# First normalization of a two-layer transformer block: rows of blocks 2 to 7 scaled and both turned halves copied by ScalarE, spread over six heads per block

## The chip, the cores and the metric

One NeuronCore of one Trainium2 chip runs the whole program. The metric is the device time of one execution in microseconds. A kernel is timed in several executions, and one more execution is taken with the hardware profiler; all rows below come from that one.

## What is computed

Two layers, each attention plus a mixture of experts on a normalized input, over 8 sequences of 512 tokens of width 256 (4096 rows). Cut to what matters here:

```python
def _layernorm(x, axis=-1, eps=1e-05):
    m = jnp.mean(x, axis=axis, keepdims=True)
    v = jnp.var(x, axis=axis, keepdims=True)
    return (x - m) / jnp.sqrt(v + eps)

# layer 0: 16 heads of 16, causal softmax over 512 tokens; 8 experts, 2 per token, plus a shared one
xn = _layernorm(x)
x = x + _L0_attn_ref(xn, Wq, Wk, Wv, Wo) + _L0_ffn_ref(xn, Wg, Wu, Wd, W1, W2)
# layer 1: gated recurrent attention over the sequence; 8 experts, 2 per token
xn = _layernorm(x)
x = x + _L1_attn_ref(xn, ...) + _L1_ffn_ref(xn, ...)
```

The change touches only the first `_layernorm`.

## The kernel before

The 4096 rows stay in on-chip memory (`ACC`) as 8 blocks of 4 tiles of 128 rows; block b is sequence b. Each sequence has two groups of eight heads, so the layer-0 attention is one loop over 128 heads, numbered by `idx`, in 16 groups `n = idx // 8`. After it come the layer-0 experts, the second layer's attention, and its experts.

The order of the attention stage is written out by hand. `attention_order` (it calls `attention_places` and `ln0_steps`) makes one list of steps, and every engine walks through that list and takes its own part of each step, strictly in order. For `idx` from -11 to 134 a turn holds, in this order: `scoresT` of head idx (TensorE computes the turned scores into banks 3 to 5, ScalarE takes the exponentials in two pieces, GpSimd masks them), the steps of `attention_places`, `scores` of head idx+11 (TensorE into banks 0 to 2, VectorE takes row maxima), `values` every fourth turn (TensorE, always into PSUM bank 6, copied out by ScalarE), and then one entry of `ln0_steps` or, when those are used up, one step of the expert routing (`route` 0 to 19 on VectorE, then 64 scatters on GpSimd). TensorE holds one head of each kind at a time: `scoresT` of a head waits for the exponentials of the head before it, `scores` for the maxima of the head before it.

The other steps of a turn repeat every eight heads: with k the group number, `project` (queries and keys of a later group, TensorE, then ScalarE and VectorE split the result) at turns 8k+2 and 8k+3, `unscaleT` at 8k+2, `scale` at 8k+1 and 8k+5 (TensorE turns, VectorE divides by the sums), `split` and `maxrow` at 8k+5 (VectorE cuts the maxima into three parts, TensorE turns them), and `output` or `project_v` at 8k+6 and 8k+7. `values` stands at 8k+4 and 8k+8.

The first normalization of blocks 0 and 1 comes ahead of the loop. For blocks 2 to 7 `ln0_steps` gives one step per turn, five turns a block: `norm` (VectorE `norm0`, L1924 to L1937: a reciprocal, then four scalings of 128x256 from `ACC` into `xn0`; SyncE L685 to L687 then stores the block to `XN`), `xt0` and `xt1` (TensorE `xt`, L1419 to L1425, turns half c of the block with four transposes; ScalarE L1139 to L1142 copies half 0 into `xnT`, VectorE L1939 to L1942 copies half 1), `logits` and `logitsT` (TensorE L1431 to L1444, VectorE copies at L1949 and L1954). The means and roots of blocks 2 to 7 are there before the loop reaches them. So block b has `norm` at turn 5b-15, `xt0` at 5b-14, `xt1` at 5b-13, `logits` at 5b-12, `logitsT` at 5b-11, and the routing starts at turn 25. All blocks from 2 on share one buffer `xn0`, so the scaling of block b waits until block b-1 is turned and stored.

PSUM banks for these short results come from `attention_banks`: a ring of four banks up to turn 0, and from turn 0 on (`two_banks`) a ring of banks 7 and 6, where each `xt0`, `xt1`, `logits`, `logitsT`, `project`, `project_v`, `maxrow`, `scale`, `unscaleT` and `output` takes the next one in turn. TensorE waits (`take`) until the last use of that bank is read. `values` always takes 6.

Of the kernel before, what the change touches and what calls it, by code (L numbers as in the profile page):

```python
# [45 lines left out]
def ln0_steps():  # L46

    yield []
    yield []
    yield [("stats", 6)]  # L50
    yield []
    yield [("stats", 7)]
    yield [("root", 2)]
    for b in range(2, NB):
        for kind in ("norm", "xt0", "xt1", "logits", "logitsT"):
            yield [(kind, b)]
# [245 lines left out]
def build(nc, t, out):  # L302
    ctx = ExitStack()
    with ctx:
# [261 lines left out]
        root = sem("root")  # L566
        normed = sem("normed")
        bank = {k: sem(f"bank{k}_read") for k in (4, 5, 6, 7)}
        turned = sem("xn_turned")
# [82 lines left out]
        def logits_read(b):  # L652

            return (bank[7], f4[3] + 2) if b == NB - 1 else (bank[6], f4[2] + 2 * b + 2)

        def rooted0(b):
            return b + 1 if b < 2 else 4


        def sync(sp):  # L660
# [24 lines left out]
            def norm0(b):  # L685
                sp.wait_ge(normed, 2 * b + 2)
                sp.dma_start(xnd[b], xn0[b]).then_inc(xn_out[b % 2], 16)  # L687
# [54 lines left out]
            for kind, *a in plan0:  # L742
                if kind == "norm":
                    norm0(*a)
                    if a[0] == 0:
                        late_loads()
                elif kind == "low":
                    split_out(*a)
# [359 lines left out]
        def scalar(act):  # L1108
# [29 lines left out]

            def xt0(b):  # L1139
                bk, use = banks0["xt0", b]  # L1140
                act.wait_ge(turned, 2 * b + 1)
                act.activation(xnT[:, 0, 512 * b:512 * b + 512], ps(bk, 0, 512), ACT.Copy).then_inc(bank[bk])  # L1142

# [70 lines left out]
            for kind, *a in plan0:  # L1214
                if kind == "stats" and a[0] >= 4:
                    stats0(*a)
                elif kind == "root":
                    root0(*a)
                    if a[0] == 0:
                        heads_last()  # L1220
                elif kind == "xt0":
                    xt0(*a)
                elif kind == "project":
                    project(*a)
                elif kind == "project_v":
                    project_v(*a)
                elif kind == "maxrow":
                    maxrow(*a)
                elif kind == "scoresT":
                    scoresT(*a)  # L1230
                elif kind == "values":
                    values(*a)
                elif kind == "shared_gelu":
                    shared_up(*a)
                elif kind == "first_gelu":
                    first_gelu(*a)
                elif kind == "first_down":
                    first_down(*a)
                elif kind == "unscaleT":
                    unscaleT(*a)  # L1240
                elif kind == "route" and a[0] == 0:
                    act.wait_ge(r_shift, 1)
                    act.activation(RR[0].A, RR[0].A, ACT.Exp).then_inc(r_exp)
# [168 lines left out]
        def tensor(pe):  # L1412
# [6 lines left out]
            def xt(b, c):  # L1419
                pe.wait_ge(normed, 2 * b + 2)  # L1420
                pe.wait_ge(cst_in, 32)
# [489 lines left out]
        def vector(dve):  # L1911
# [12 lines left out]
            def norm0(b):  # L1924
                dve.wait_ge(root, rooted0(b))
                dve.reciprocal(RS[:, 4 * b:4 * b + 4], RS[:, 4 * b:4 * b + 4]).then_inc(normed)
                dve.wait_ge(normed, 2 * b + 1)
                if b == 2:
                    dve.wait_ge(xn_out[0], 16)
                elif b > 2:  # L1930
                    dve.wait_ge(xn_out[(b - 1) % 2], 16 * ((b - 1) // 2 + 1))
                if b >= 2:
                    dve.wait_ge(turned, 2 * b)
                for j in range(4):
# [3 lines left out]

            def xt1(b):  # L1939
                bk, use = banks0["xt1", b]  # L1940
                dve.wait_ge(turned, 2 * b + 2)
# [572 lines left out]
```

## Time and profile before

| | us |
|---|---|
| median of 3 runs | 1647.87 (1644.03 to 1649.47) |
| profiled execution, its own time | 1642.28 |
| span of its trace | 1640.5 |

Over the span TensorE's matmuls are busy 1536.9 us (94%), VectorE 861.1 us (52%), ScalarE 733.3 us (45%), GpSimd 713.8 us (44%). The attention loop runs from about 34 us to 499 us, the layer-0 experts follow. The page names engines PE (TensorE matmul), PEld (its weight loads), DVE (VectorE), ACT (ScalarE), POOL (GpSimd), SP (SyncE). `L1936` is line 1936 of the kernel. In a row of the timeline the bracket at the end holds the idle time of the engine ahead of the piece and what ended it; in a row that holds several instructions the form printed is that of the first. In the windows each engine has its busy time with the instruction count in brackets; PEclk is the granted TensorE clock as a share of 2.4 GHz, DMA the busy share of the DMA engines. The windows of group 2 begin and end where a `values` step starts: 84.44 us is turn 4, 99.19 turn 8, then 12 at 113.64, 16 at 128.99, 20 at 144.51, 24 at 162.57, 28 at 179.57, 32 at 191.62, 40 at 216.72, 48 at 250.24.

### The profile page before, as it was taken

How to read it: one execution, taken by the hardware profiler on the slowest of the kernel's cores; microseconds unless marked ns; L12 is line 12 of the kernel's file. 1: busy time of each engine (PE TensorE's matmuls, PEld its weight loads, DVE VectorE, ACT ScalarE, POOL GpSimd, SP SyncE). 2: the span in 40 equal slices, each digit the busy share in tenths (PEclk: the TensorE clock that was granted, in tenths of full speed). 3: DMA queues.
4: the chain of work that ended last, by engine and by line, in shares of the span. 5: the costliest groups of instructions: out<-in, count | busy, mean ns of one | idle time of the engine just before them, and what ended most of it. 6: DMA issues, size and time to landing. Idle time of an engine off the chain costs nothing.

```text
span 1640.5 us, 32489 instructions
## 1 busy us (share of the span) xinstructions
PE 1536.9 (94%) x10874; PEld 1180.9 (72%) x10874; DVE 861.1 (52%) x2424; ACT 733.3 (45%) x1923; POOL 713.8 (44%) x815
## 2 busy tenths in 40 slices
PE   5888989999999999999988799998999999999997
PEld 3445445555547999998655467767999899999996
DVE  5777897787822444442577778874322122222220
ACT  4544545555551232333556466644333333334332
POOL 3132336676532555553810467753333333333332
PEclk9899999999999999999998999999999999999999
DMA  8534324435306444444622386467333333333331
GB/s 271 126 115 110 79 73 98 104 94 102 83 4 240 108 113 114 113 114 130 204 92 67 103 219 105 79 105 290 59 56 52 51 56 54 55 58 59 53 55 23
DMA packets 154640, 167.60 MB, mean 102 GB/s; under 512 B 84821, under 2 KB 132817, under 8 KB 151409
## 3 DMA queue, kind: packets, MB, share of 16 engines
q1 hardware_dynamic: 129936, 128.15, 31.5%
q0 software_dynamic: 24544, 37.38, 10.6%
q8 instruction: 94, 1.54, 0.4%
q14 instruction: 66, 0.53, 0.1%
HBM read 104.10 MB, written 44.45 MB: 91 GB/s over the span
## 4 chain that ended last, share of the span: by engine, by line
PE 78%; DVE 10%; DMA 4%; issue 3%; ACT 3%; SPq 1%; POOL 0%; another core or an unknown queue 0%; DVEq 0%; ACTq 0%; POOLq 0%
PE PS L1660 23%; PE PS L1678 22%; PE PS L1517 4%; PE PS L1453 3%; PE PS L1767 3%; DVE PS L1980 3%; PE PS L1502 3%; PE PS L1481 2%; PE PS L1634 2%; PE PS L1543 2%; PE PS L1588 2%; PE PS L1779 2%; PE PS L1463 1%; PE PS L1865 1%; DMA arena<-FD 1%
## 5 line engine op out<-in xcount | busy, mean ns | idle before, releaser
L1660 PEld LDWEIGHTS PS<-arena 128*128 128x128 f32 x3408 | 398.2, 192 | 16.3 <-DVE arena L2201 4.9
L1660 PE MATMUL PS<-arena 128*128 128x128 f32 x3408 | 405.3, 276 | 3.5 <-DVE arena L2201 3.5
L1678 PE MATMUL PS<-arena 128*128 x1704 | 392.3, 379 | 0.0
L1678 PEld LDWEIGHTS PS<-arena 128*128 128x128 f32 x1704 | 311.9, 190 | 40.1 <-issue 0.2
L1980 DVE CUSTOM_DVE_ANT_0 PS<-PS,arena 128x512 f32<-128x512 f32 (+3 forms) x512 | 235.2, 522 | 50.7 <-PE PS L1481 47.2
L995 POOL DMA_INDIRECT out<-arena x71 | 111.7, 1573 | 296.4 <-ACT arena L1272 274.0
L1262 ACT ACTIVATE arena<-PS,arena 128x128 f32<-128x128 f32 x568 | 161.8, 368 | 138.3 <-PE PS L1660 136.5
L2226 DVE COPY arena<-arena 128x8 f32 x71 | 12.2, 172 | 347.5 <-ACT arena L1262 326.3
L928 POOL TENSOR_SCALAR_AFFINE_SELECT arena<-arena 128x256 f32<-128x256 f32 x256 | 99.4, 411 | 204.0 <-ACT arena L1178 203.7
L981 POOL DMA_INDIRECT arena<-XN,arena x142 | 145.0, 1021 | 98.6 <-PE PS L1645 40.6
L1178 ACT ACTIVATE arena<-PS 128x512 f32<-128x512 f32 (+1 forms) x256 | 166.5, 705 | 42.1 <-PE PS L1502 34.4
L1272 ACT ACTIVATE arena<-PS,arena 128x256 f32<-128x256 f32 x142 | 67.3, 474 | 256.0 <-PE PS L1680 177.8
L2227 DVE COPY arena<-arena 128x1024 f32 (+1 forms) x142 | 136.5, 961 | 75.5 <-ACT arena L1254 59.4
L954 POOL DMA_INDIRECT SLOT<-arena x128 | 155.7, 1217 | 30.3 <-issue 30.3
L988 POOL DMA_INDIRECT SUM<-arena x71 | 70.2, 989 | 98.0 <-ACT arena L1272 98.0
L1481 PE MATMUL PS<-arena 96*128 96x512 bf16 (+3 forms) x512 | 100.3, 307 | 8.1 <-DVE arena L1980 5.7
L1502 PE MATMUL PS<-arena 99*128 99x512 bf16 (+3 forms) x512 | 97.5, 307 | 6.0 <-ACT arena L1178 5.3
L1254 ACT ACTIVATE arena<-PS 128x512 f32<-128x512 f32 x71 | 42.4, 597 | 115.3 <-issue 75.3
L1502 PEld LDWEIGHTS PS<-arena 99*128 99x128 bf16 x512 | 45.5, 99 | 56.7 <-issue 18.1
L2215 DVE COPY arena<-arena 128x512 uint16<-128x512 uint16 x126 | 53.7, 426 | 60.1 <-DMA arena<-XN,arena 59.1
L1481 PEld LDWEIGHTS PS<-arena 96*128 96x128 bf16 x512 | 49.1, 99 | 49.3 <-DVE arena L1980 16.5
L1517 PE MATMUL PS<-arena 128*32 128x512 f32 (+3 forms) x1024 | 75.7, 435 | 4.8 <-DVE arena L1966 3.6
(246 smaller groups left out, 2014.3 us busy)
## 6 DMA issues: line engine op xcount, KB each, us to landing
arena<-FD SPq DMA_DIRECT2D x32, 512.0 KB
arena<-in_w SPq DMA_DIRECT2D x16, 1024.0 KB
SPL<-arena SPq DMA_DIRECT2D x32, 384.0 KB, 2.6
arena<-SPL SPq DMA_DIRECT2D x64, 192.0 KB
XN<-arena SPq DMA_DIRECT2D x16, 512.0 KB, 3.0
arena<-SPL SPq DMA_DIRECT2D x64, 128.0 KB
arena<-SUM SPq DMA_DIRECT2D x16, 512.0 KB, 6.4
arena<-in_x SPq DMA_DIRECT2D x8, 512.0 KB, 6.6
```

What stands on the lines that cost most here:

```text
L954: pool.indirect_dma_start(SLOT[layer], bass.IndirectOffsetOnAxis(ap=POS[:, n, i:i + 1], axis=0), META[:, i, n, :], None).then_inc(row_out[ ...
L981: pool.indirect_dma_start(MOE[layer].xr[i % 4][:, :], None, XN, row).then_inc(tile_in[i % 4], 16)
L995: pool.indirect_dma_start(out, row, m.y[i % 3][:, :], None, compute_op=ALU.add).then_inc(y_out[i % 3], 16)
L1178: act.activation(PB[h % NPB][:, lo:hi], ps(3, lo, hi), ACT.Exp, scale=0.25).then_inc(p_made)
L1262: ins = act.activation(m.hT[i % len(m.hT)][:, 128 * f:128 * f + 128], ps(m.UPB[i % 2], 128 * f, 128 * f + 128), ACT.Gelu, bias=m.bias[i % ...
L1481: ins = pe.matmul(ps(0, o, o + w), q[0:96, j, 128 * i:128 * i + 128], k[0:96, j, 0:w], start=True, stop=True)
L1502: ins = pe.matmul(ps(3, o, o + w), k[0:99, j, 128 * kb:128 * kb + 128], q[0:99, j, 128 * kb:512], start=True, stop=True)
L1517: ins = pe.matmul(PS[32 * j:32 * j + 32, 6, 128 * kb:512], vb[:, kb, 8 * half + jj, :], PB[(8 * n + jj) % NPB][:, OFFT[kb]:OFFT[kb] + w], ...
L1660: ins = pe.matmul(o, m.now[i % 2][:, c * F + 128 * f:c * F + 128 * f + 128], m.xt[i % 2][:, 128 * c:128 * c + 128], start=(c == 0), stop=( ...
L1678: ins = pe.matmul(to, m.hT[i % len(m.hT)][:, 128 * c:128 * c + 128], m.WD[:, bass.ds(e * (nf * 256) + c * 256, 256)], start=(c == 0), stop ...
L1980: dve.tensor_tensor_reduce(sc, sc, MASK[:, 384 - 128 * r:512], -1.0, -NEG, ALU.add, ALU.min, NM[n % 2][:, r, j:j + 1]).then_inc(s_max)
L2227: dve.tensor_copy(m.now[i % 2][:, :], m.WU[:, bass.ds(e * m.wrow, m.wrow)]).then_inc(w_staged)
```

## The change

Blocks 0 and 1 stay as they are. For blocks 2 to 7 VectorE's `norm0` keeps the reciprocal and adds one small operation that makes NB1 = -mean x 1/deviation; the four scalings are now ScalarE activations (`ACT.Identity` with per-row scale and bias), two per turn in two turns, called `scaled` 0 and 1. ScalarE also copies half 1 of the turned block. A block now takes six turns instead of five: `norm` and `scaled` 0 at 6b-17, `scaled` 1 at 6b-16, `xt0` at 6b-15, `xt1` at 6b-14, `logits` at 6b-13, `logitsT` at 6b-12; the routing starts at turn 31. The waits for the store and for the turning of the block before move from VectorE to ScalarE. TensorE and SyncE wait for the new semaphore `scaled0` instead of `normed`, and SyncE stores a block at `scaled` 1.

```diff
@@ ln0_steps
     for b in range(2, NB):
-        for kind in ("norm", "xt0", "xt1", "logits", "logitsT"):
+        yield [("norm", b), ("scaled", b, 0)]
+        yield [("scaled", b, 1)]
+        for kind in ("xt0", "xt1", "logits", "logitsT"):
             yield [(kind, b)]
@@ build
+        def normed0(b):
+            return (normed, 2 * b + 2) if b < 2 else (scaled0, 2 * b - 2)
@@ sync
             def norm0(b):
-                sp.wait_ge(normed, 2 * b + 2)
+                sp.wait_ge(*normed0(b))
                 sp.dma_start(xnd[b], xn0[b]).then_inc(xn_out[b % 2], 16)
...
-                if kind == "norm":
+                if kind == "norm" and a[0] < 2:
                     norm0(*a)
...
+                elif kind == "scaled" and a[1] == 1:
+                    norm0(a[0])
@@ scalar
-            def xt0(b):
-                bk, use = banks0["xt0", b]
-                act.wait_ge(turned, 2 * b + 1)
-                act.activation(xnT[:, 0, 512 * b:512 * b + 512], ps(bk, 0, 512), ACT.Copy).then_inc(bank[bk])
+            def xt(b, c):
+                bk, use = banks0[f"xt{c}", b]
+                act.wait_ge(turned, 2 * b + 1 + c)
+                act.activation(xnT[:, c, 512 * b:512 * b + 512], ps(bk, 0, 512), ACT.Copy).then_inc(bank[bk])
+
+            def scaled(b, half):
+                act.wait_ge(normed, 2 * b + 2)
+                act.wait_ge(turned, 2 * b)
+                if b == 2:
+                    act.wait_ge(xn_out[0], 16)
+                else:
+                    act.wait_ge(xn_out[(b - 1) % 2], 16 * ((b - 1) // 2 + 1))
+                for j in (2 * half, 2 * half + 1):
+                    i = 4 * b + j
+                    ins = act.activation(xn0[b][:, j, :], ACC[:, i, :], ACT.Identity, bias=NB1[:, i:i + 1], scale=RS[:, i:i + 1])
+                ins.then_inc(scaled0)
...
-                elif kind == "xt0":
-                    xt0(*a)
+                elif kind == "xt0" or kind == "xt1" and a[0] >= 2:
+                    xt(a[0], int(kind[2]))
+                elif kind == "scaled":
+                    scaled(*a)
@@ tensor
             def xt(b, c):
-                pe.wait_ge(normed, 2 * b + 2)
+                pe.wait_ge(*normed0(b))
@@ vector
                 dve.wait_ge(normed, 2 * b + 1)
-                if b == 2:
-                    dve.wait_ge(xn_out[0], 16)
-                elif b > 2:
-                    dve.wait_ge(xn_out[(b - 1) % 2], 16 * ((b - 1) // 2 + 1))
                 if b >= 2:
-                    dve.wait_ge(turned, 2 * b)
+                    dve.scalar_tensor_tensor(NB1[:, 4 * b:4 * b + 4], MV[:, 4 * b:4 * b + 4, 0], -1.0, RS[:, 4 * b:4 * b + 4], ALU.mult, ALU.mult).then_inc(normed)
+                    return
...
             def xt1(b):
+                if b >= 2:
+                    return
```

## Rows read from the trace of the kernel before

**Rows 1.** The profile's page: span and busy time by engine

```profile
span 1640.5 us, 32489 instructions
PE 1536.9 (94%) x10874; PEld 1180.9 (72%) x10874; DVE 861.1 (52%) x2424; ACT 733.3 (45%) x1923; POOL 713.8 (44%) x815
```

**Rows 2.** Windows: length, then busy PE, PEld, DVE, ACT, POOL; PEclk, DMA, GB/s

```profile
84.44:99.19 14.75, 11.98 (x82) 6.79 (x82) 11.64 (x48) 7.53 (x12) 4.31 (x10) 0.78 0.45 141
...
144.51:162.57 18.06, 15.96 (x112) 10.55 (x113) 12.24 (x48) 6.32 (x11) 3.99 (x9) 0.81 0.34 104
162.57:179.57 17.00, 14.48 (x82) 6.43 (x82) 12.06 (x49) 7.62 (x14) 4.32 (x9) 0.90 0.30 76
...
216.72:250.24 33.52, 27.89 (x174) 15.50 (x173) 28.91 (x106) 14.32 (x25) 12.60 (x21) 0.90 0.30 71
...
287.22:311.73 24.51, 23.27 (x168) 13.26 (x169) 18.99 (x77) 14.28 (x25) 16.13 (x27) 1.00 0.45 98
```

**Rows 3.** Timeline of TensorE, turns 1 to 8: start, length, line, idle before

```profile
70.49 0.38 PE L1502 MATMUL PS<-arena 99*128 99x512 bf16 x1 [1.03 <-ACT arena L1178]
...
72.78 1.12 PE L1424 MATMUL PS<-arena 128*128 128x128 f32 x4 [0.64 <-DVE arena L1936]
...
87.61 0.30 PE L1444 MATMUL PS<-arena 128*128 128x128 f32 x1 [0.81 <-ACT arena L1184]
...
93.03 1.11 PE L1424 MATMUL PS<-arena 128*128 128x128 f32 x4 [1.96 <-DVE arena L1936]
...
96.07 1.06 PE L1424 MATMUL PS<-arena 128*128 128x128 f32 x4
```

**Rows 4.** The same timeline, turns 12 to 45

```profile
116.80 0.63 PE L1424 MATMUL PS<-arena 128*128 128x128 f32 x4 [0.80 <-ACT arena L1184]
...
118.36 0.60 PE L1525 MATMUL PS<-arena 128*128 128x128 f32 x4
...
121.46 0.64 PE L1437 MATMUL PS<-arena 128*32 128x128 f32 x16 [2.10 <-DVE arena L2004]
...
150.97 1.09 PE L1424 MATMUL PS<-arena 128*128 128x128 f32 x4 [2.10 <-DVE arena L2004]
...
174.46 3.65 PE L1453 MATMUL PS<-arena 128*128 128x512 f32 x4 [0.35 <-DVE arena L1966]
...
240.17 0.60 PE L1489 MATMUL PS<-arena 128*24 128x128 bf16 x4 [2.11 <-DVE arena L1993]
```

**Rows 5.** The same timeline, in a stretch without normalization or routing on VectorE

```profile
311.73 2.36 PE L1517 MATMUL PS<-arena 128*32 128x512 f32 x32 [0.36 <-DVE arena L1966]
...
317.73 1.97 PE L1543 MATMUL PS<-arena 128*128 128x256 f32 x8 [0.38 <-DVE arena L2004]
319.54 0.71 PE L1502 MATMUL PS<-arena 99*128 99x512 bf16 x4
```

**Rows 6.** Timeline of VectorE around the normalization of block 7

```profile
146.28 1.38 DVE L1936 TENSOR_SCALAR arena<-arena 128x256 f32<-128x256 f32 x4
```

**Rows 7.** Groups by line, 60 to 200 us: VectorE and ScalarE forms that the change concerns

```profile
L1178 ACT ACTIVATE arena<-PS 128x768 f32<-128x768 f32 x35 | 28.4, 812 | 0.1
...
L1936 DVE TENSOR_SCALAR arena<-arena 128x256 f32<-128x256 f32 x20 | 7.5, 435 | 0.2
...
L1942 DVE COPY arena<-PS 128x512 f32<-128x512 f32 x6 | 4.1, 685 | 2.6 <-PE PS L1424 2.6
```

**Rows 8.** Timeline of ScalarE: the second layer's normalization, the same form of activation

```profile
791.42 2.08 ACT L1314 ACTIVATE arena<-arena 128x256 f32<-128x256 f32 x4 [2.21 <-DVE arena L2273]
793.40 1.05 ACT L1199 ACTIVATE arena<-PS 128x512 f32<-128x512 f32 x2
794.47 1.28 ACT L1378 ACT_TABLE_LOAD   x1
```

**Rows 9.** The lines of the second layer's per-row scaling and its small VectorE operation

```profile
L1314 ACT ACTIVATE arena<-arena x32: 584/588/602, 791.4 to 862.6; 128x256 f32<-128x256 f32 x32
...
L2273 DVE SCALAR_TENSOR_TENSOR arena<-arena x8: 161/164/2452, 789.8 to 860.9; 128x4 f32<-128x4 f32 x8
```

More of the change, by code:

```diff
@@ L567, in build @@
         normed = sem("normed")
+        scaled0 = sem("scaled0")
         bank = {k: sem(f"bank{k}_read") for k in (4, 5, 6, 7)}
```

## The prediction

> **What bounds the kernel now.** I read the page first [rows 1]: matmuls are busy 94% of the span, so time can only come from gaps of TensorE or from its clock. Then windows over the attention loop [rows 2]. A stretch with neither normalization nor routing needs 24.51 us for eight heads, with TensorE busy 23.27 of it at full clock. While blocks 4 to 7 are normalized, the four-head windows take 14.75, 18.06 and 17.00 us; all six from turn 4 to turn 28 take 179.57 - 84.44 = 95.1 us, where three quiet periods would take 73.5. Granted clock falls there too: 0.78, 0.81, 0.90. Third, TensorE's own timeline, for what ended its gaps. At 93.03 it waited 1.96 us for the scalings of block 4 (L1936), at 72.78 0.64 us for those of block 3 [rows 3]. At 121.46 and 150.97 it waited 2.10 us each for `scale` on VectorE (L2004), the second time behind the scalings of block 7, which stand 4 us earlier in VectorE's queue [rows 4, 6]. At 87.61 and 116.80 it waited 0.8 us for ScalarE's copy of the `values` bank, since a short step had drawn bank 6 too [rows 3, 4].
>
> A gap costs twice. After the gap before 93.03, one turning of a half with a `scoresT` and a `scores` takes 96.07 - 93.03 = 3.04 us; the same three take 118.36 - 116.80 = 1.56 us elsewhere [rows 3, 4]. That is 1.2 instead of 2.4 GHz, and it lasts two such rounds, so it costs some 3.0 us on top of the gap. The same follows the gaps before 72.78, 150.97 and 240.17 (0.6, 2.1, 2.1 us), and at 174.46 four matmuls of projections take 3.65 us, some 1.8 of it the slow clock if that doubles them too, after gaps of 0.3 [rows 3, 4]. So VectorE's queue at normalization is on the path although VectorE is busy 52% over the span.
>
> **What the change removes, adds and moves.** VectorE loses per block four scalings of 0.435 us by the mean (1.38 us in a row, they overlap) and one copy of 0.685 us, and gains one small operation of 0.16 us [rows 6, 7, 9]: some 1.9 us less per block, 11.5 us over six. ScalarE gains 2.08 us for four scalings of this very form, and about 0.53 us for the copy, as two such copies in a row take 1.05 [rows 8]: 2.6 us per block, 15.7 us over six. It is busy 6.3 to 7.6 us in those windows of 14.8 to 18.1 us [rows 2], so there is room. TensorE's and SyncE's instructions stay the same in number; they move to later turns.
>
> *ScalarE's new wait.* ScalarE now waits, at turn 6b-17, for a VectorE operation queued behind the maxima of that turn, and the exponentials of the next head are queued behind it. Let TensorE end that turn's `scores` at t. VectorE ends its share by t + 2.3 at most (9.3 us for four heads, being 11.64 busy less the scalings and the copy [rows 2, 7]), the two small operations end at t + 2.7, two scalings at t + 3.7, the next exponentials (0.81 and some 0.55 us) at t + 5.1. TensorE meanwhile does the next `scoresT` and, held by the same maxima, the next `scores`, and is through at about t + 2.5. What covers the rest is the long step of the next turn. The turns 6b-16 are 2, 8, 14, 20 and 26 for blocks 3 to 7, and each holds one: `project` at 2 and 26, `project_v` at 14 (1.8 us as at 319.54 - 317.73 [rows 5]), `values` at 8 and 20 (2.4 us [rows 5]). That leaves a gap of about 0.2 to 0.8 us per block, mostly shorter than those before. Without that cover it would be 2 to 2.6 us.
>
> *Sum, turns 4 to 28.* Three quiet periods are 73.5 us. Heads 6 and 7 have no `output` or `project_v` yet, less 2 x 1.8 = 3.6: 69.9. In turns 5 to 8 VectorE's 9.3 us are then longer than TensorE's 12.3 - 3.6 = 8.7, and with small gaps I take 1.3 more: 71.2. TensorE's normalization work in these turns is 8 turned halves of about 0.5 us (0.63 less the overlap with the next piece), 4 `logits` of about 0.58 (0.64 less overlap) and 4 short turnings of 0.1 [rows 4]: 6.7, together 77.9. The new waits above take 0.5 us in each of five places: 2.5. That TensorE never falls to 1.2 GHz in this stretch is too much to ask; before it did at 93, 151 and 174 us, and I leave one such fall of 3.0 in. That makes 83.4, so 11.7 us less than 95.1. Without any fall it is 14.7; with all three left, 5.7.
>
> *What is paid back.* One turned half, a `logits` and a short turning of block 7 move behind turn 28: 1.2 us. Routing step 0, a chain between VectorE and ScalarE, moves from turn 25 to turn 31. Before, its window lost 17.00 - 14.48 = 2.5 us in gaps and those 1.8 us in slow projections [rows 2, 4]; not all of it is the chain's. Between 0.7 and 4.2, I take 2.0 us. Together 3.2.
>
> *Before turn 4.* The scalings of block 2 leave VectorE just before the first maxima are cut, for which TensorE waits. This is worth between nothing and their 1.38 us [rows 6]; I take 1.0, since at block 4 the whole length showed.
>
> *Banks.* From turn 0 on the short results alternate between 7 and 6. `logitsT` of block 2 now falls into turn 0, so all later steps draw the other bank. Before, the second `project` of a period had bank 6, and `values`, always bank 6, waited 0.36 us for VectorE to read it [rows 5]. That wait recurs each eight heads. After, the last user of bank 6 ahead of that `values` is `unscaleT`, read long before. Twelve periods from turn 32 on give at most 4.3 us; as 0.38 us at L1543 [rows 5] shows that VectorE is close behind at other places, I take 3.5, and nothing as the other end.
>
> *Routing steps 15 to 19* now lie at turns 46 to 50, not 40 to 44. Their window takes 33.52 us, 9.0 more than a quiet period, part of it a fall of the clock after 240.17 [rows 2, 4]. VectorE's work in them is unchanged. I take no change, with 3 us to either side. The 64 scatters end at turn 114 instead of 108, still before the loop's end, so they cost nothing; if they ran past it, six of them of about a turn each would show.
>
> The sum: 1.0 + 11.7 + 3.5 - 3.2 = 13.0 us. The profiled execution of 1642.3 becomes 1629.3; it was 5.6 us below the median of 1647.9, so on the median I predict **1634.9 us**.
>
> **A rule against the change.** The row of the same form shows 0.588 us for a ScalarE scaling [rows 9], VectorE's takes 0.435 us [rows 7], so the moved work grows by a third. The Trainium skill, page "ScalarE: Activation LUTs", section "Rules for kernel authors", says just this: additions and multiplications belong on VectorE. Were ScalarE's time on the path, the 24 scalings would cost 24 x 0.15 = 3.7 us more instead of saving 10. By the windows it is not, so the sum does not follow the rule.
>
> **The rivals.**
>
> *More goes than I think.* The falls at 93, 151 and 174 all vanish, and that before 72.78, which follows gaps of 1.03 us on ScalarE and 0.64 us on the scalings [rows 3], goes too. That is 6 us more: about 1629.
>
> *Only the direct gaps go.* Other gaps take over as the cause of the slow clock, as the heads have a lead of only one over VectorE. What remains is 1.96 + 0.64 + about 1.4 at 150.97 and part of the bank effect: 5.5 us, less 3.2 paid back, or 1642 to 1646. For it: two of the 2.1 us waits end at L2004, not at the scalings. Against: that L2004 is late by the scalings in the same queue.
>
> *ScalarE's wait becomes the gap (slower).* At each 6b-17 the exponentials of the next head stand behind VectorE, TensorE waits 2 to 2.6 us (the figure without cover) and falls to half clock for another 3.0: about 5.3 us for each of five blocks, 26 us against 13. That gives 1661. It decides from 13.0 / 5 = 2.6 us per block on. For it: gaps of 2 us and a slow clock do go together in every case above. Against: a long TensorE step follows each of the five places.
>
> *A table load per scaling.* If `ACT.Identity` were not in the table that the exponentials use, each turn with scalings would add two loads of 1.28 us [rows 8]. Ten turns in the loop with half of it on the path are 13 us, which cancels the gain: 1648 to 1660. The row shows the scalings and then a Gelu with no load between them, but no row shows them between exponentials.
>
> *It does not do what it says.* If the scalings of a block were late for its `xt0`, TensorE would wait there as before. They end over a turn ahead of it, so this has no chance of its own.
>
> **Chances.** The forecast, 1630 to 1641: 0.52. More: 0.12. Direct gaps only: 0.24. ScalarE's wait: 0.09. Table loads: 0.03. About 0.3%, or 4.9 us, is what a measurement of this kernel can tell from no change, so faster means below 1643.0. From the forecast, the larger gain and half of the third case: 0.76. Same, 1643.0 to 1652.8: the other half of the third and some of the last two, 0.15. Slower: 0.09. The range takes in the bounds of routing, banks and clock falls: 1624 to 1647.
>
> **What the profile would show.** No L1936 row after block 1, and ScalarE rows of 128x256 in pairs, without a table load beside them. TensorE's turnings at full clock, with no gap over 1 us before them. The six windows from turn 4 to 28 together near 83 us, a quiet period near 24.2 us, and no wait of `values` for VectorE's L1966 in it. The routing window would still be some 9 us too long. I am wrong if TensorE's gaps are ended by the exponentials right after the `scaled` turns, if the clock in the windows is still about 0.8, or if the quiet period is unchanged.

## The result, and the profile after

The changed kernel takes **1625.07 us** (median of 4 runs, 1620.84 to 1626.41); the kernel before, run beside it, 1645.95 us (median of 4, 1639.79 to 1649.47). The ratio is 0.989 with a 95% interval of 0.986 to 0.992; by the ratio the gain is 18 us, 13 to 23 by its interval, so the 13.0 that I had predicted lie at its edge. The profiled execution took 1625.28 us, that of before 1642.28. I had predicted 1634.9: the direction was right, the gain between the medians was 20.9 us instead of 13.0. The forecast's own band, 1630 to 1641, did not hold it; the range, 1624 to 1647, did.

The page of the kernel after answers to [rows 1] (busy time, its share of the span, instructions):

```profile
span 1623.5 us, 32501 instructions
PE 1525.4 (94%) x10874; PEld 1171.9 (72%) x10874; DVE 847.0 (52%) x2400; ACT 747.1 (46%) x1953; POOL 714.1 (44%) x815
```

VectorE lost 14.1 us and ScalarE gained 13.8, near the 11.5 and 15.7 that I had worked out. TensorE executes the same 10874 matmuls in 11.5 us less: most of the 17 us by which the span is shorter is clock, not gaps.

The windows of after, turns 4 to 28 in steps of four heads, then turns 28 to 32, the window with routing (turns 44 to 52), and a quiet one (turns 56 to 64); columns as in [rows 2]:

```profile
77.58:89.75 12.17, 9.84 (x95) 5.07 (x94) 10.05 (x44) 6.41 (x12) 4.37 (x10) 1.00 0.38 118
...
117.71:131.78 14.07, 12.77 (x103) 6.88 (x102) 9.81 (x39) 7.49 (x13) 4.12 (x9) 1.00 0.54 111
131.78:147.13 15.35, 12.96 (x113) 8.38 (x113) 11.65 (x46) 9.71 (x18) 4.12 (x9) 1.00 0.44 132
147.13:160.49 13.36, 12.76 (x86) 6.40 (x85) 10.22 (x41) 9.14 (x17) 3.86 (x9) 1.00 0.44 108
160.49:174.50 14.01, 12.33 (x110) 8.16 (x109) 10.76 (x43) 7.75 (x14) 4.38 (x10) 1.00 0.33 96
...
211.04:243.14 32.10, 27.23 (x173) 14.09 (x173) 29.96 (x124) 15.13 (x26) 9.57 (x19) 0.95 0.34 88
255.12:279.00 23.88, 23.15 (x169) 13.03 (x168) 18.94 (x77) 14.01 (x25) 16.15 (x26) 1.00 0.46 103
```

The third column from the right is the granted clock. It is 1.00 in every window up to turn 32, where [rows 2] had 0.78, 0.81 and 0.90. Turns 4 to 28 in one window, before and after:

```profile
84.44:179.57 95.13, 81.69 (x590) 46.27 (x590) 70.21 (x275) 44.51 (x74) 25.32 (x54) 0.91 0.38 106
```

```profile
77.58:160.49 82.91, 73.98 (x589) 41.61 (x588) 61.38 (x247) 52.91 (x93) 24.70 (x55) 1.00 0.44 118
```

The 12.2 us are 7.7 of TensorE's busy time and 4.5 of idle time. The busy time is the slow clock: either window holds eight turned halves and four `logits`, since block 3's second half and its `logits` move into it at turn 4 as block 7's move out at turn 28; only one short turning (0.3 us) is missing. ScalarE is busy 52.9 of 82.9 us, 64%, and VectorE 74% in either kernel.

TensorE's timeline of after, every idle stretch over 0.4 us between turns 4 and 29 (start, length, line, idle before):

```profile
84.06 0.64 PE L1459 MATMUL PS<-arena 128*32 128x128 f32 x16 [1.68 <-DVE arena L2025]
...
99.26 0.63 PE L1446 MATMUL PS<-arena 128*128 128x128 f32 x4 [1.07 <-DVE arena L1987]
...
127.65 0.30 PE L1466 MATMUL PS<-arena 128*128 128x128 f32 x1 [1.07 <-DVE arena L1987]
...
134.62 0.38 PE L1524 MATMUL PS<-arena 99*128 99x512 bf16 x1 [0.47 <-ACT arena L1198]
...
138.72 0.63 PE L1446 MATMUL PS<-arena 128*128 128x128 f32 x4 [1.68 <-DVE arena L2025]
...
166.98 0.64 PE L1459 MATMUL PS<-arena 128*32 128x128 f32 x16 [1.68 <-DVE arena L2025]
```

L2025 is `scale` (L2004 before), L1987 the subtraction in `low` (L1966 before), L1198 the exponentials (L1178 before). The scalings end no gap any more, the 1.96 of [rows 3] is gone, and so are the 0.8 us waits for bank 6. What is left over 0.4 us are waits for VectorE to read a bank, but for one: a gap of 0.47 us ends at the exponentials behind the `scaled` step. ScalarE around that step:

```profile
132.90 1.09 ACT L1161 ACTIVATE arena<-arena 128x256 f32<-128x256 f32 x2 [1.51 <-DVE arena L1951]
133.90 1.27 ACT L1198 ACTIVATE arena<-PS 128x512 f32<-128x512 f32 x2
```

It sat idle 1.51 us for the small operation (L1951), 1.57, 1.98, 1.23 and 2.10 at the four other places that the trace names, and there is no table load between the scalings (Identity) and the exponentials.

Seen from the start of the `values` step of each fourth head, after is ahead of before by 6.9 us at turn 4, 19.1 at turn 28, 17.1 at turn 32, 19.8 at turn 52, 21.9 at turn 104 and 21.9 at the end of the attention loop (first matmul of L1634 before, 499.0 us; L1656 after, 477.1). From there to the end of the span, code that the change does not touch, before takes 1141.5 us and after 1146.4. So 4.9 us of the profiled pair's gain go missing there, of which the experiments say more. The 21.9 us are 6.9 before turn 4, 12.2 in turns 4 to 28, 2.0 paid back in turns 28 to 32, and 4.8 from turn 32 on (307.4 against 302.6 us).

### The profile page after: what moved, and what is told of

Its sections match the earlier page's. It is cut to its first block, busy times and chain, and to the rows that moved or that the text cites. A ratio compares the mean times of both kernels' runs of the same rounds, so it can differ in the third digit from the quotient of the medians.

```text
span 1623.5 us, 32501 instructions
## 1 busy us (share of the span) xinstructions
PE 1525.4 (94%) x10874; PEld 1171.9 (72%) x10874; DVE 847.0 (52%) x2400; ACT 747.1 (46%) x1953; POOL 714.1 (44%) x815
## 4 chain that ended last, share of the span: by engine, by line
PE 66%; issue 9%; DVE 9%; POOL 8%; DMA 3%; ACT 2%; SPq 2%; another core or an unknown queue 0%; DVEq 0%; POOLq 0%; ACTq 0%
PE PS L1682 23%; PE PS L1700 23%; POOL SLOT L962 6%; DVE PS L2001 3%; PE PS L1475 3%; PE PS L1539 3%; PE PS L1656 2%; PE PS L1524 2%; PE PS L1610 2%; PE PS L1503 2%; PE PS L1565 2%; SPq L715 1%; POOL arena L1064 1%; PE PS L1485 1%; DMA arena<-SPL 1%
## 5 line engine op out<-in xcount | busy, mean ns | idle before, releaser
L2247 DVE COPY arena<-arena 128x8 f32 x71 | 12.2, 172 | 346.6 <-ACT arena L1284 334.6
L1198 ACT ACTIVATE arena<-PS 128x512 f32<-128x512 f32 (+1 forms) x256 | 166.0, 704 | 33.6 <-PE PS L1524 25.2
L2397 DVE TENSOR_TENSOR_SCAN arena<-arena 128x1024 f32<-128x1024 f32 x32 | 73.0, 2281 | 9.6 <-DMA arena<-FD 9.6
```

Of the source, the lines that this page charges most:

```text
L1198: act.activation(PB[h % NPB][:, lo:hi], ps(3, lo, hi), ACT.Exp, scale=0.25).then_inc(p_made)
```

## Experiments

Each ran beside the kernel before on its own chip, in four groups on four chips (ring_before, ring_after, six_turns_vector, five_turns_scalar; changed_again, xt1_vector, norm_early, woven; changed_third, scaled_twice, six_turns_scalar; woven_late); the ratio is to the kernel before on that chip, with its 95% interval. The kernels changed_again and changed_third are the changed kernel itself, run again. The table puts the profiled executions side by side. "Busy" and "idle" are TensorE's, in turns 4 to 28; "loop end" is the time of the first matmul behind the attention loop, "rest" the span less that.

| kernel | ratio | turn 4 | turns 4-28 | busy | idle | loop end | rest |
|---|---|---|---|---|---|---|---|
| before | 1 | 84.4 | 95.13 | 81.69 | 13.44 | 499.0 | 1141.5 |
| ring_before | 0.995 [0.993, 0.997] | 81.8 | 92.58 | 80.65 | 11.93 | 488.5 | 1137.4 |
| six_turns_vector | 0.995 [0.992, 0.998] | 81.9 | 88.81 | 78.58 | 10.23 | 488.3 | 1149.7 |
| five_turns_scalar | 0.9965 [0.994, 0.999] | 85.4 | 93.84 | 79.69 | 14.15 | 496.0 | 1140.9 |
| six_turns_scalar | 0.993 [0.991, 0.995] | 79.8 | 88.25 | 75.88 | 12.37 | 484.2 | 1146.1 |
| scaled_twice | 0.995 [0.993, 0.997] | 80.6 | 90.02 | 76.51 | 13.51 | 488.6 | 1144.9 |
| ring_after | 0.9945 [0.991, 0.998] | 79.2 | 85.90 | 74.13 | 11.77 | 483.3 | 1140.5 |
| after | 0.989 [0.986, 0.992] | 77.6 | 82.91 | 73.98 | 8.93 | 477.1 | 1146.4 |
| changed_again | 0.989 [0.985, 0.992] | 80.1 | 82.91 | 73.98 | 8.93 | 479.2 | 1144.6 |
| changed_third | 0.992 [0.989, 0.995] | 79.2 | 83.96 | 75.42 | 8.54 | 481.1 | 1146.6 |
| xt1_vector | 0.990 [0.987, 0.993] | 79.4 | 84.60 | 75.40 | 9.20 | 482.4 | 1150.4 |
| norm_early | 0.990 [0.986, 0.993] | 77.8 | 83.93 | 75.20 | 8.73 | 479.1 | 1150.3 |
| woven | 0.990 [0.986, 0.994] | 80.7 | 80.94 | 74.49 | 6.45 | 481.0 | 1145.7 |
| woven_late | 0.987 [0.985, 0.990] | 79.3 | 80.94 | 74.48 | 6.46 | 478.1 | 1141.0 |

The last column answers one question at once. The rest takes 1137.4 to 1150.4 us in one and the same code, in no order that follows an edit. The 4.9 us "given back" by after are within that, and are no effect of the change that these runs can show.

**Which bank the short results take: ring_before and ring_after.** One line in either kernel:

```
-            ring = [7, 6]
+            ring = [6, 7]
```

> The kernel before, but the ring of two banks begins with 6 instead of 7 at turn 0, so every short step of the loop draws the other bank. Bank theory: the quiet period of eight turns falls from 24.5 to 24.2 us, the values step no longer waits 0.36 us for the second projection to be read, and 2 to 4 us go over the whole loop (1642 to 1644 if before is 1646). If the bank has no part in it, the quiet period stays at 24.5 and the time is unchanged. The normalization stretch from turn 4 to 28 stays above 92 us in either case.

> The changed kernel with the ring begun with 6, which gives the later steps the banks of before. Bank theory: quiet period back at 24.5 us, 2 to 4 us slower than the changed kernel, the stretch from turn 4 to 28 still near 83 us. If the banks were behind the vanished clock falls, the stretch would go back above 90 us.

Before gains 0.5% by it, 6.9 us at the median where 2 to 4 were expected, and a quiet period falls from 24.51 [rows 2] to 23.90 us:

```profile
279.00:302.90 23.90, 23.46 (x171) 13.04 (x169) 18.84 (x76) 14.42 (x25) 16.20 (x27) 1.00 0.49 101
```

Behind turn 28 the kernel with the swap is 5.3 us shorter, all of it idle time of TensorE (20.7 to 15.5 us).

After loses by it in the trace; at the median the loss is not clear, since the interval of ring_after, 0.991 to 0.998, touches those of the changed kernel. Its waits for ScalarE's copy of the `values` bank are back, five in the timeline of ring_after, four in turns 4 to 28 and one at 168.26, and so is the wait of `values` for L1987 in the quiet period:

```profile
110.03 0.30 PE L1466 MATMUL PS<-arena 128*128 128x128 f32 x1 [0.81 <-ACT arena L1204]
...
123.77 0.63 PE L1446 MATMUL PS<-arena 128*128 128x128 f32 x4 [0.81 <-ACT arena L1204]
...
296.91 2.36 PE L1539 MATMUL PS<-arena 128*32 128x512 f32 x32 [0.37 <-DVE arena L1987]
```

Against changed_again, turns 4 to 28 are 3.0 us longer, 2.8 of it idle time. That lies among the normalization, where I had not looked for it. From turn 28 to the loop's end the difference is 2.0 us (318.2 against 316.2), but there the idle time is the same (18.5 against 18.4), and changed_third takes 318.0, so those 2.0 cannot be put down to the banks. The quiet period of ring_after is 24.2 us, not the 24.5 that I had expected: in after it is 23.9 and 24.2 by turns, with small waits for the exponentials (0.38 and 0.23 us in the longer ones) in place of the one for L1987. So the banks carry 3 to 5 us of the change as seen from after. In before's order of steps the same swap brings more, 2.6 us in turns 4 to 28 and 5.3 behind them.

**Moving without spreading, and spreading without moving.** The change does two things: ScalarE instead of VectorE, and six turns for a block instead of five. In six_turns_vector the kernel before only gets an empty turn:

```
     for b in range(2, NB):
-        for kind in ("norm", "xt0", "xt1", "logits", "logitsT"):
+        yield [("norm", b)]
+        yield []
+        for kind in ("xt0", "xt1", "logits", "logitsT"):
             yield [(kind, b)]
```

> The kernel before, but six turns a block: an empty turn between the scalings, still on VectorE, and the first turning. Steps, turns and banks are those of the changed kernel, only the engine of the scalings and of the second copy is the old one. Queue theory (VectorE's work is what counts): 3 to 9 us below before, the turn 4 to 28 stretch near 90 us, since TensorE no longer waits for the scalings by name but for the maxima queued behind them. Spreading theory (only the distance counts): 15 to 21 us below before, the stretch near 83 us.

In five_turns_scalar the kernel after has both halves in the turn of the small operations, so five turns again:

```
-        yield [("norm", b), ("scaled", b, 0)]
-        yield [("scaled", b, 1)]
+        yield [("norm", b), ("scaled", b, 0), ("scaled", b, 1)]
```

> The changed kernel with five turns a block: both halves of the scalings follow on ScalarE in the turn of the norm step, so turns and banks are those of before and only the engine differs. Queue theory: 10 to 18 us below before, the turn 4 to 28 stretch at 83 to 88 us. Spreading theory: 0 to 5 us below before, since the first turning waits for the scalings as before, now for 2.1 us of ScalarE behind VectorE; the stretch above 90 us.

The two ratios, 0.995 and 0.9965, have overlapping intervals. Either part alone is worth 0.35 to 0.5%, where the whole is worth 0.8 to 1.1% by the three ratios of the changed kernel. In turns 4 to 28 spreading saves 6.3 us and moving 1.3, where both together (with the split) save 12.2. Neither theory held in both experiments: six_turns_vector came out as the queue theory had it (88.8 us, 7.4 us below before at the median), five_turns_scalar as the spreading theory had it (93.8 us). With all 24 scalings off VectorE and the distance as before, TensorE waits for them on ScalarE instead, at the very places of [rows 3], and longer, and 0.81 us at block 5 as well. From the timeline of five_turns_scalar:

```profile
73.69 1.12 PE L1445 MATMUL PS<-arena 128*128 128x128 f32 x4 [1.56 <-ACT arena L1160]
...
94.66 1.11 PE L1445 MATMUL PS<-arena 128*128 128x128 f32 x4 [2.68 <-ACT arena L1160]
```

1.11 us for a turned half is the slow clock (0.63 at full). These gaps came from a block's turning standing one turn behind its scalings, whoever did them. With a turn between them no gap ends at the scalings in six_turns_vector, but those for `scale` stay, with the slow clock behind them:

```profile
145.66 1.09 PE L1426 MATMUL PS<-arena 128*128 128x128 f32 x4 [2.11 <-DVE arena L2006]
146.54 1.27 PE L1504 MATMUL PS<-arena 99*128 99x512 bf16 x4
```

Note that six_turns_vector holds the bank effect too, since the sixth turn is what shifts the ring. That is a rival for the turn itself: ring_before, which has the banks and no sixth turn, has the same ratio, 0.995, and reaches the loop's end at 488.5 us against 488.3. The 3.8 us that six_turns_vector is ahead of it in turns 4 to 28 are paid back in turns 28 to 32 (16.2 against 12.0 us). So no run shows a gain in time from the turn alone. The profiled execution of six_turns_vector is also the slowest of its ten, 1639.71 us where their median is 1630.78.

**What the split into halves is worth: six_turns_scalar.** After, with the distance kept and the split undone:

```
-        yield [("norm", b), ("scaled", b, 0)]
-        yield [("scaled", b, 1)]
+        yield [("norm", b), ("scaled", b, 0), ("scaled", b, 1)]
+        yield []
```

> The changed kernel, a block's steps still over six turns, but both halves of the scalings are yielded in the turn of the small operations and the second turn is empty: all four scalings of a block in one row on ScalarE. Theory A (the distance to the first turning is what matters, the split is free): no wait of TensorE for the scalings, the exponentials behind four scalings come about 1 us later than behind two, so a gap of 0.5 to 1.3 us at five places: turns 4 to 28 in 85 to 89 us, median +2 to +6 over the changed kernel. Theory B (the split into two turns is what makes ScalarE's share harmless): the exponentials behind four scalings are late by 1.6 to 2.7 us, as TensorE waited in the kernel with five turns, and the clock falls behind them: turns 4 to 28 in 92 us or more, median +8 or more.

Here the rival "ScalarE's wait becomes the gap" comes true in part. Against changed_third on the same chip, turns 4 to 28 take 4.3 us more, and the exponentials behind four scalings hold TensorE at each block of the loop, 0.75, 0.33, 0.90, 1.46 and 0.93 us at blocks 3 to 7. Its timeline:

```profile
116.78 0.38 PE L1524 MATMUL PS<-arena 99*128 99x512 bf16 x1 [0.90 <-ACT arena L1198]
...
139.52 0.38 PE L1524 MATMUL PS<-arena 99*128 99x512 bf16 x1 [1.46 <-ACT arena L1198]
...
143.60 1.04 PE L1446 MATMUL PS<-arena 128*128 128x128 f32 x4 [1.68 <-DVE arena L2025]
```

That is theory A, at the upper end of its 85 to 89 us. Of the 4.3 us, 3.8 are idle time. At the median the two are 1631.19 and 1629.37 us with overlapping intervals, so the split's worth is shown by the gaps, not by the times. Set beside six_turns_vector, this kernel also says what moving the scalings and the copy is worth once there are six turns: 88.81 to 88.25 us, with 2.7 us less busy and 2.1 us more idle time. So, taken in this order and from single profiles, the 12.2 us fall into 6.3 for the sixth turn (banks included), 0.6 for moving and 5.3 for the split. Over the whole loop moving shows more: its end comes at 484.2 us against 488.3, with 6.3 us less busy and 2.2 us more idle time. Whether the split would do as much on VectorE was not tried.

**More work on ScalarE: scaled_twice.** Each pair of scalings of blocks 3 to 7 is done a second time into a scratch area that nothing reads:

```
+                if b > 2:
+                    act.wait_ge(extra, 4 * (b - 3) + 2 * half)
+                    for j in (2 * half, 2 * half + 1):
+                        i = 4 * b + j
+                        act.activation(view(route0 + 2088 + 256 * (j % 2), 256), ACC[:, i, :], ACT.Identity, ...).then_inc(extra)
```

> The changed kernel; for blocks 3 to 7 ScalarE does each pair of scalings a second time, into a scratch area that nothing reads (20 activations of 128x256 more, about 1.09 us per pair, ten pairs, 11 us of ScalarE in turns 1 to 26). The output stays that of the reference. Theory A (cover): ScalarE has room in these turns, and only the exponentials right behind a pair are late, under the long step of the next turn: the pair now costs 1.1 us more there, which the cover of 1.8 to 2.4 us takes for some blocks and not for others: turns 4 to 28 longer by 0 to 3 us, median +0 to +3. Theory B (ScalarE's time is on the path once its queue is on it, as the rule on additions and multiplications would have it): nearly all of the 11 us show, turns 4 to 28 longer by 8 to 11 us, median +8 or more, more still with falls of the clock.

Neither theory held as put: turns 4 to 28 are 6.1 us longer than in changed_third, between the 0 to 3 and the 8 to 11 (5.0 idle, 1.1 busy), and the median is 5.5 us above it. TensorE's gaps at the exponentials are those of six_turns_scalar to 0.01 us, and one more of 0.90 us at 99.05, behind the second pair of block 4:

```profile
118.52 0.38 PE L1530 MATMUL PS<-arena 99*128 99x512 bf16 x1 [0.90 <-ACT arena L1204]
...
141.65 0.38 PE L1530 MATMUL PS<-arena 99*128 99x512 bf16 x1 [1.46 <-ACT arena L1204]
```

The two kernels share the first turn, four activations behind the small operation, and differ in the second, none against four. So the second pair has room for twice its work at four blocks of five. The first pair, which stands behind ScalarE's wait, has next to none: 1.09 us added there comes out as 0.75 to 0.99 us of gap at four blocks of five, and as 0.33 at the fifth. The cover that I had counted on, the long step of TensorE's next turn, exists, and the change uses it up.

**Parts of the change done otherwise.** The second copy of a turned half back on VectorE (xt1_vector: `xt` on ScalarE for `xt0` alone, and no early return in VectorE's `xt1`), and the small operations a turn ahead of the scalings (norm_early):

```
-        yield [("norm", b), ("scaled", b, 0)]
+        yield [("scaled", b, 0)]
...
+        yield [("logitsT", b)] + ([("norm", b + 1)] if b + 1 < NB else [])
```

> The changed kernel once more, as the measure for its neighbours on this chip. If the clock falls are chance for a given set of gaps, its trace shows the same gaps as the first one (1.68 us at turns 5, 21 and 29, 1.07 us at 10 and 18) to 0.1 us, while the number of slow stretches up to turn 32 may be 0 to 2 instead of 0. If they follow from the gaps alone, there is no slow stretch again. Time 8 to 20 us below before.

> The changed kernel with the second copy (half 1 of the turned block) back on VectorE. Queue theory: VectorE has 0.6 us more in each of six turns and waits there for the turning, so the gaps before the next maxima grow: 1 to 4 us slower than the changed kernel, the turn 4 to 28 stretch at 84 to 87 us. If the copy is of no account, the stretch stays at 83 us and the time within 1 us.

> The changed kernel with VectorE's two small operations one turn earlier than the first scalings, so ScalarE no longer waits 1.2 to 2.0 us for them with the exponentials queued behind. If that wait costs TensorE only its covered remainder, as forecast, 0 to 1.5 us go: the gap of 0.47 us at turn 21 disappears, the rest stays. If ScalarE's wait were a hidden main cost, 3 to 8 us go.

In time neither can be told from the changed kernel. In the trace the copy's price shows: with it on VectorE, `scale` is late by 2.10 instead of 1.68 us at turn 5 (86.34) and at turn 29 (170.95), 0.42 us each, and both times the clock fell. With the small operations a turn early, ScalarE's wait and the gap of 0.47 are gone (0.22 us is left of the waits, at one place), but the gap for `scale` at turn 21 grew from 1.68 to 2.10 us, and there too the clock fell. The work had only changed places in VectorE's queue. From xt1_vector:

```profile
86.34 1.08 PE L1459 MATMUL PS<-arena 128*32 128x128 f32 x16 [2.10 <-DVE arena L2023]
87.36 1.25 PE L1524 MATMUL PS<-arena 99*128 99x512 bf16 x4
```

**Short steps out of the crowded turns: woven and woven_late.** The remaining 1.68 and 1.07 us gaps stand where a short step of the normalization falls in a turn that already takes both banks (8k + 5 with `scale`, 8k + 2 with a `project`). In woven the steps of all blocks are rearranged so that none takes a bank there, for instance

```
+    yield [("logitsT", 4)]
+    yield []
+    yield [("xt0", 5)]
+    yield [("xt1", 5), ("norm", 6)]
+    yield [("scaled", 6, 0), ("logits", 5)]
+    yield [("scaled", 6, 1), ("logitsT", 5)]
+    yield []
```

> The changed kernel with its steps rearranged: turning, logits steps never in turns 8k+2 and 8k+5, where they draw a bank that VectorE reads late, the next block's scalings already beside the logits steps, the small VectorE operations a turn ahead. If the remaining gaps of 1.68 us (three) and 1.07 us (two) come from the bank drawn in those turns, they vanish, and the stretch from turn 4 to 28 goes from 83 to 78 to 80 us; 3 to 7 us below the changed kernel. If they come from VectorE's queue as such, new gaps of the same size stand before other steps, and the time is unchanged.

> The changed kernel as it is, for comparison on the same chip with the three beside it. Both theories: median near 1625.5 us, turns 4 to 28 in 82.9 us, no slow clock of TensorE between 41 and 236 us, first exponential-bound and `scale` gaps at the same turns as in the two profiles so far.

> The changed kernel with the steps of blocks 3 to 7 woven as in the kernel `woven` (none that takes a bank in turns 8k+2 and 8k+5, the next block's scalings between a block's steps), but block 2 and the first half of block 3 stand where the changed kernel has them, and two empty turns at the end leave routing at its turns. Theory A (the rest of TensorE's gaps in turns 4 to 28 are those of the banks, and what made the first woven kernel no better lay outside of them, at 70 us and at 218 us): turns 4 to 28 in 80 to 82 us, the gaps of 1.57 at 70 us and of 2.28 at 218 us gone, median 2 to 4 us below the changed kernel, so a ratio of about 0.987 where the changed kernel's three were 0.989, 0.989 and 0.992. Theory B (each placement brings gaps of its own): other waits of 1 us and more take their place, turns 4 to 28 in 83 us or more, median as the changed kernel's.

The gaps of 1.68 and 1.07 us are gone, in both, and in their place stand 0.81 us for the copy of the `values` bank, at three turns, and 0.38 for `scale`. From woven_late:

```profile
85.79 0.64 PE L1490 MATMUL PS<-arena 128*32 128x128 f32 x16 [0.38 <-DVE arena L2056]
...
93.24 0.63 PE L1477 MATMUL PS<-arena 128*128 128x128 f32 x4 [0.81 <-ACT arena L1235]
```

Turns 4 to 28 take 80.94 us, as theory A of woven_late said, 2.0 less than after; the 78 to 80 expected of woven were missed. The window holds more work than that of after, one turned half and one `logits` (about 1.2 us). The changed kernel's third run missed its expectation in part: its gaps are the expected ones, but the clock fell at turn 5 and again behind turn 29, and turns 4 to 28 took 83.96 us. The 1.57 us gap at 70 us, which woven had, is gone in woven_late, whose first blocks stand as in after. The other gap of woven, 2.28 us ahead of routing's first matmul (218.58 there) with the clock falling behind it, is still there (215.54). The edit failed to test it: routing starts right behind the last `logitsT`, which stands two turns earlier than in after, so the two empty turns at the end were never reached. Its median, 1624.76 us, is the lowest of all, but its interval, 0.985 to 0.990, overlaps those of the changed kernel. Whether it is faster stays open.

## Why the prediction came out as it did

*What bounds the kernel: right.* The loss lay in the gaps around normalization and in the clock behind them. All of [rows 2 to 4]'s slow stretches in turns 4 to 28 are gone in after; changed_third has one new one, at turn 5.

*Turns 4 to 28: 83.4 predicted, 82.91 measured, by errors that cancel.* The 2.5 us for ScalarE's new waits came out as 1.6: one gap of 0.47 us and five of 0.19 to 0.23. The 3.0 us for a remaining fall of the clock came out as nothing in two profiles and as 1.4 us of busy time in the third. But the 77.9 us of undisturbed work were too little: two waits of 1.68 us for `scale` and two of 1.07 us for `low`, 5.5 us, stood where I had allowed 1.3 of small gaps. I had seen the 2.10 us waits for `scale` [rows 4] and had put them down to the scalings ahead of it in VectorE's queue. With all scalings gone from that queue it is still 1.68 us late, since the short step needs the bank that `scale` reads, and `scale` stands behind the turn's maxima. The step "L2004 is late by the scalings" holds for 0.42 us of it at turn 21. At turns 5 and 29 these 0.42 us belong to the copy of the second half, since they come back in xt1_vector, which has no scaling on VectorE. What 0.42 us are worth was missed as well, as the clock below shows.

*Before turn 4: mis-sized.* Predicted 1.0 us, 6.9 in the first pair. Two profiles with before's order of work and VectorE's scalings (before, ring_before) reach turn 4 at 81.8 and 84.4 us; five with after's (after, changed_again, changed_third, ring_after, xt1_vector) at 77.6 to 80.1. The means, 83.1 and 79.1, are 4.0 apart; some 3 of the 6.9 may thus be chance. Of the 4.0, 1.2 are work put off, which the sum left out: the second half of block 3 and its `logits` stood at turns 2 and 3 before and stand at turns 4 and 5 after. The sum counted the same work of block 7 as paid back at turn 28 and never took it as gained here. I had counted the scalings' 1.38 us, and had moved to a rival that before loses the clock behind the gap before 72.78, though I had described it myself.

*Banks: right cause, but its place and size hold only in part.* Predicted 3.5 us, all behind turn 32. Seen from after (ring_after against changed_again) they are 3.0 in turns 4 to 28, and behind turn 28 2.0 that are no idle time and within what the changed kernel's own profiles differ. Seen from before (ring_before) they are 2.6 and 5.3. The pair itself gained 4.8 us from turn 32 on, 2.6 of it up to turn 56, in and around the routing, for which I had predicted nothing.

*Paid back: 3.2 predicted, 2.0 measured* (12.05 to 14.01 us in turns 28 to 32). *Routing: no change predicted*, 33.52 [rows 2] to 32.10 us measured, inside the 3 us to either side.

*The attribution was the real fault.* The prediction spoke of VectorE's load and costed that. five_turns_scalar shows that the load alone is worth 0.35%, between 0.1 and 0.6. The sixth turn, which I took for mere bookkeeping, is needed too: it puts a turn between scalings and turning, makes room for the split, and shifts the ring of banks. But by itself it brings no more time than the banks do (six_turns_vector against ring_before). The parts work together, and they do so largely through the clock. TensorE executes 2975 or 2976 matmuls up to the loop's end in every profile. It is busy with them for 438.9 to 441.9 us in before, ring_before, six_turns_vector and five_turns_scalar, and for 429.1 to 433.8 in the ten profiles whose kernels have both the scalings on ScalarE and a block's first scalings at least two turns ahead of its turning. No profile of one group lies in the other. One reason can be read at the waits for `scale` up to turn 32. Where such a gap was 2.10 us, the granted clock was below 1.00 in the 6 us from its end in nine cases of ten; where it was 1.68 us, in seven of 23. That both go together is shown; that the 0.42 us are the cause is an inference, since the kernels differ in other things too.

*The rivals.* "More goes than I think" is what came, with even more than its 1629. "Only the direct gaps go" is out: the clock stays up in the windows. Its doubt about L2004 was right all the same: the waits for it stayed at 1.68 us. "ScalarE's wait becomes the gap" is not what the change does, but its mechanism is real, and the margin is about one pair of scalings (six_turns_scalar, scaled_twice); I gave its price, 2.0 to 2.6 us a block, too high for that case (0.33 to 1.46). "A table load per scaling" is out by the row at 132.90. The rule of the Trainium skill (page "ScalarE: Activation LUTs", section "Rules for kernel authors") that additions and multiplications belong on VectorE holds per operation here too, 0.596 us a scaling in after against 0.435 [rows 7]. For the kernel's time it does not decide: the move alone still gained 0.35% (five_turns_scalar), less than I had costed, with ScalarE on TensorE's path there, and the whole change gained more with its gaps at the exponentials held to 1.6 us in turns 4 to 28.

What stays open: how much of the 20.9 us at the median is the clock's chance, and how the gain divides among the turn, the move and the split, for which no kernel has the split on VectorE. One kernel's runs spread that wide themselves, and of the three ratios measured for the changed kernel the mildest, 0.992, would be 13 to 14 us.

## What to carry to other kernels

When a step is late, ask both how many turns lie between its producer and its consumer and what stands ahead of it in its queue: here emptying the queue alone gave 0.35% and one more turn alone 0.5%, all of which the banks may account for, where the whole gave 0.8 to 1.1%. Adding a turn shifts whatever alternates by count, buffers and banks above all; work out on which turn each falls after the change, and swap the ring's start as an experiment of one line, which by itself gave 0.5% in the kernel before. And put work behind a wait only as much as the other engine's long step covers: two activations cost little there (gaps up to 0.47 us) and four cost 0.33 to 1.46 us a block.

## What the runs showed of the hardware

The same gap is followed by a slow clock in one execution and not in another. At the gap of 1.68 us at turn 5, changed_third runs on at 1.25 us for four `scoresT` matmuls:

```profile
85.66 0.94 PE L1459 MATMUL PS<-arena 128*32 128x128 f32 x16 [1.68 <-DVE arena L2025]
86.53 1.25 PE L1524 MATMUL PS<-arena 99*128 99x512 bf16 x4
```

and changed_again, with the same gap at the same place, at 0.72:

```profile
86.58 0.64 PE L1459 MATMUL PS<-arena 128*32 128x128 f32 x16 [1.68 <-DVE arena L2025]
87.16 0.72 PE L1524 MATMUL PS<-arena 99*128 99x512 bf16 x4
```

Likewise the 1.96 us gap of [rows 3] is followed by a turned half of 0.66 us in ring_before, where before had 1.11. Two consequences, which I had not expected. The gaps of the changed kernel in turns 4 to 32 repeat over its three profiles to about 0.01 us, while the time of a kernel does not: 29 runs of the kernel before on one chip lie between 1627.2 and 1646.5 us. And a gap costs its own length in every one of them, and the clock behind it only in some, the longer gap more often (nine of ten waits for `scale` of 2.10 us, seven of 23 of 1.68 us), so that a single profile's windows over- or understate an edit by one or two falls of up to 3 us each. A decomposition into busy and idle time, as in the table, keeps the two apart.
